# A graph network's last layer: fp32r halves for its weights, GpSimd for their products, PSUM for the running maximum

## The chip, the cores and the metric

The kernel runs on one core of one Trainium2 chip. The metric is the device time of one execution in microseconds (us); lower is better. TensorE multiplies matrices, VectorE and ScalarE work elementwise, GpSimd (POOL in the profile) too but without PSUM, and SyncE issues DMAs. Each engine runs its own instructions in order and waits for the others by semaphores.

## What is computed

Four graph layers work on 1354 nodes with 256 features. Each is `x = x + layer(relu(layernorm(x)), adj)`; the adjacency matrix `adj` is 1354 x 1354, F32, mostly zero. Layer 0 is softmax attention with `adj` added to the scores, layer 1 gated attention over neighbours, layer 2 a mean over neighbours. The change concerns layer 3:

```python
S = S + eye(n)                         # S is adj
h = x @ W
scores = where(S > 0, h @ U @ h.T, -inf)
att = softmax(scores, axis=-1)
return (S * att) @ h
```

## The kernel before

Nodes are cut into NB = 11 blocks of 128 (the last has 74). `adj` is stored transposed, so a tile has 128 neighbours (j) on the partitions and up to 512 target nodes in its columns. The targets form NG = 3 groups of 512, 512 and 330 columns, that is 4, 4 and 3 blocks. So there are NT = 33 tiles, numbered n = 11 * group + j. `slot3(n)` is the place in SBUF in which tile n's scores lie.

What layer 3 does for a tile, in the order of the data:

- TensorE, `score`: six fp32r matmuls make the scores in one of two PSUM banks. Layers 0 and 3 keep their operands as a high half, rounded to fp32r, and a low half, the rest; a product takes three matmuls (hi*hi, hi*lo, lo*hi; `products`, L309 to L311).
- VectorE, `add3` (L1322): masks with adj, negates, and writes the slot.
- VectorE, `running` (L912, L915): the running minimum of negated scores (the maximum, turned round) over the 11 tiles of a group, in `m_sb` in SBUF. When a group is complete, TensorE transposes `m_sb` (`turn_max`, L1490), VectorE reduces it (`top`, L894), and TensorE spreads the result over a PSUM bank (`spread_max`, L1499).
- VectorE, `shift` (L923): subtracts the group's maximum, from PSUM.
- ScalarE, `exp3` (L808): the exponential, in place.
- VectorE, `times_s` (L1330): times adj, into one of three places of `w_ring`, F32.
- GpSimd, `add_total` (L453): adds the exponentials of a group's tiles up in `total`. The first tile of a group is copied there by ScalarE (L812).
- TensorE, `aggregate3` (L1798): one F32 matmul for each of the group's blocks, weights times values, accumulated over the 11 tiles of the group. The profile has two records for each such F32 matmul.

At the end of a group `add_up` (L1814) sums `total` over partitions by matmuls with ones, and `out3` (L1338, L1344) divides and adds to x; SyncE stores each block.

The values `h @ W` are made in F32 in `v3` by ScalarE, from PSUM (`values`, L514). The layer's beginning is mixed with the end of layer 2 (`out2`, `turn_y`, `project2`) and with the normalisation of x.

The order is written by hand in a loop over steps s on each engine. In step s TensorE makes score s; VectorE takes it in `add3(s)` and shifts tile n at step `shift_step(n)`, which is n + 11 for the first group and n + 12 for the others. `times_s(n)` comes one step later and `aggregate3(n)` two steps later. The step count is NT + LAG3. Scores end with step 32; what comes behind is the tail, tiles 20 or so to 32. Layer 0 has the same shape of loop, with its weights in halves already: `weighted` (L1512, L1513 for the high part, L1517 for the low part) does three fp32r matmuls for each block.

## Time and profile before

| | |
|---|---|
| runs of the kernel | 415.62, 415.60, 414.38 us; median 415.6 |
| profiled execution, its own time | 415.22 us |
| its span in the trace | 413.4 us |
| busy of the span | TensorE 95%, VectorE 80%, ScalarE 53%, GpSimd 22% |
| mean granted TensorE clock | 0.996 of full speed |
| DMA queues | mean 34 GB/s; nearly idle after the first 40 us |

The span is what the trace covers, from the first instruction to the last; the time of the same execution has some 1.8 us more around it. The trace gives a start and a duration for each instruction. Matmuls overlap, so their spacing, not their duration, says what one costs.

### The profile page before, as it was taken

To read this page: it belongs to the slowest core of one execution; us is meant where nothing else is said; L and a number is where in the kernel's file an instruction comes from. 1 tells how busy PE (TensorE), PEld (TensorE's weight loads), DVE (VectorE), ACT (ScalarE), POOL (GpSimd) and SP (SyncE) were. 2 spreads that over 40 slices of the span, in tenths; PEclk is the share of its full clock that TensorE was granted. 3 is DMA by queue.
4 is the path that set the end of the run, shared out by engine and by line. 5 is a ranking of instruction groups with operands and counts; after the bars stand their busy time and mean duration, and the time that the engine had idled before them with its cause. 6 is when DMAs were issued, how large, how long until landed. Compare 5 with 4: busy or idle time off the path is not lost.

```text
span 413.4 us, 7338 instructions
## 1 busy us (share of the span) xinstructions
PE 394.8 (95%) x2534; PEld 355.2 (86%) x2534; DVE 329.1 (80%) x761; ACT 220.7 (53%) x454; POOL 89.5 (22%) x105
## 2 busy tenths in 40 slices
PE   8999999999899999999989999999999999999995
PEld 6787779989889989999989989997887788889863
DVE  4799789989895756998998989765758778798763
ACT  1453799975777567786777893254232311122330
POOL 1191000000110233233031001051010034324552
PEclk9999999999999999999999999999999999999998
DMA  8993000000000001000000000000000000010011
GB/s 249 376 377 120 2 0 2 2 0 2 1 2 0 2 0 52 2 2 0 3 2 0 2 1 2 2 1 2 0 2 0 2 1 0 2 51 2 0 52 33
DMA packets 10300, 13.96 MB, mean 34 GB/s; under 512 B 644, under 2 KB 7192, under 8 KB 10264
## 3 DMA queue, kind: packets, MB, share of 16 engines
q1 hardware_dynamic: 10264, 13.49, 9.6%
q8 instruction: 21, 0.34, 0.4%
q14 instruction: 15, 0.12, 0.1%
HBM read 12.10 MB, written 1.39 MB: 33 GB/s over the span
## 4 chain that ended last, share of the span: by engine, by line
PE 72%; DVE 17%; issue 6%; ACT 2%; POOL 1%; DVEq 0%; POOLq 0%; ACTq 0%
PE ps L1798 9%; PE ps L1517 9%; PE ps L1512 8%; PE ps L1513 8%; PE ps L309 6%; PE ps L311 6%; PE ps L310 6%; PE ps L1431 4%; PE ps L1725 3%; PE ps L1724 3%; PE ps L1754 2%; DVE m_sb L915 2%; PE ps L1536 2%; DVE s_sb L885 2%; DVE p_lo L929 1%
## 5 line engine op out<-in xcount | busy, mean ns | idle before, releaser
L1512 PE MATMUL ps<-v_hi,p_hi 128*128 128x258 f32 (+3 forms) x242 | 64.5, 297 | 1.1 <-DVE x_sb L941 0.7
L1513 PE MATMUL ps<-v_lo,p_hi 128*128 128x258 f32 (+3 forms) x242 | 61.0, 281 | 0.0
L1798 PE MATMUL ps<-v,w_ring 128*128 128x256 f32 (+3 forms) x242 | 58.0, 385 | 1.3 <-DVE w_ring L1330 0.8
L1798 PEld LDWEIGHTS ps<-v,w_ring 128*128 128x128 f32 (+3 forms) x242 | 43.2, 186 | 11.1 <-DVE w_ring L1330 4.5
L376 POOL TENSOR_TENSOR mr_all<-mr_all,mhalf 128x4 f32<-128x4 f32 (+1 forms) x12 | 13.3, 1106 | 173.6 <-DVE mr_all L847 173.6
L1512 PEld LDWEIGHTS ps<-v_hi,p_hi 128*128 128x128 f32 (+3 forms) x242 | 44.6, 184 | 3.5 <-ACT p_hi L520 1.6
L808 ACT ACTIVATE s_sb<-s_sb 128x512 f32<-128x512 f32 (+3 forms) x30 | 17.3, 575 | 53.9 <-DVE s_sb L923 53.9
L1513 PEld LDWEIGHTS ps<-v_lo,p_hi 128*128 128x128 f32 (+3 forms) x242 | 44.7, 185 | 0.5
L453 POOL TENSOR_TENSOR total<-total,s_sb 128x512 f32<-128x512 f32 (+3 forms) x27 | 30.6, 1134 | 65.2 <-DVE w_ring L1330 65.2
L1517 PE MATMUL ps<-v_hi,p_lo 128*128 128x258 f32 (+3 forms) x242 | 40.4, 285 | 2.1 <-DVE p_lo L929 1.7
L923 DVE TENSOR_TENSOR s_sb<-s_sb,ps 128x512 f32<-128x512 f32 (+3 forms) x63 | 38.4, 611 | 0.8 <-PE ps L1499 0.7
L1517 PEld LDWEIGHTS ps<-v_hi,p_lo 128*128 128x128 f32 (+3 forms) x242 | 32.5, 185 | 3.4 <-DVE p_lo L929 2.5
L915 DVE TENSOR_TENSOR m_sb<-m_sb,s_sb 128x512 f32<-128x512 f32 (+3 forms) x51 | 33.0, 646 | 0.9
L413 POOL TENSOR_TENSOR mid_lo<-adjT_sb,mid_hi 128x512 fp32r<-128x512 f32 (+2 forms) x16 | 20.6, 1289 | 51.4 <-ACT mid_hi L628 51.4
L1512 PE MATMUL ps<-big_hi,mid_hi 128*128 128x258 f32 (+3 forms) x121 | 31.7, 293 | 0.0
L1513 PE MATMUL ps<-big_lo,mid_hi 128*128 128x258 f32 (+3 forms) x121 | 30.3, 281 | 0.0
L309 PE MATMUL ps<-mid_hi,v_hi 128*128 128x512 f32 (+3 forms) x66 | 28.7, 434 | 1.0 <-DVE s_sb L1322 1.0
L637 ACT ACTIVATE p_hi<-s_sb,minus_r 128x512 fp32r<-128x512 f32 (+3 forms) x33 | 22.1, 671 | 11.2 <-PE ps L1517 4.5
L1105 DVE SCALAR_TENSOR_TENSOR s_sb<-s_sb,sx 128x512 f32<-128x512 f32 (+3 forms) x33 | 26.0, 789 | 1.2
L1322 DVE SCALAR_TENSOR_TENSOR s_sb<-adjT_sb,ps 128x512 f32<-128x512 f32 (+3 forms) x30 | 18.5, 616 | 10.3 <-PE ps L311 10.0
L309 PE MATMUL ps<-mid_hi,big_hi 128*128 128x512 f32 (+3 forms) x66 | 25.2, 382 | 0.8 <-DVE mid_lo L866 0.8
L520 ACT ACTIVATE p_hi<-s_sb 128x512 fp32r<-128x512 f32 (+3 forms) x33 | 19.0, 576 | 13.0 <-DVE s_sb L923 12.8
(228 smaller groups left out, 1049.5 us busy)
## 6 DMA issues: line engine op xcount, KB each, us to landing
adjT_sb<-in_adjT_dram SPq DMA_DIRECT2D x1, 2816.0 KB, 16.5
adjT_sb<-in_adjT_dram SPq DMA_DIRECT2D x3, 768.0 KB, 9.7
adjT_sb<-in_adjT_dram SPq DMA_DIRECT2D x1, 1815.0 KB, 20.9
out_dram<-x_sb SPq DMA_DIRECT2D x10, 128.0 KB
x_sb<-in_x_dram SPq DMA_DIRECT2D x2, 512.0 KB, 5.2
adjT_sb<-in_adjT_dram SPq DMA_DIRECT2D x1, 512.0 KB, 11.4
rows_sb<-in_rows_dram SPq DMA_DIRECT2D x1, 385.0 KB, 11.0
s_sb<-in_wq_dram SPq DMA_DIRECT2D x1, 256.0 KB, 3.9
```

The source lines that it names most:

```text
L309: eng.matmul(out_ap, lhs[0], rhs[0], start=first, stop=False)
L310: eng.matmul(out_ap, lhs[0], rhs[1], start=False, stop=False)
L311: return eng.matmul(out_ap, lhs[1], rhs[0], start=False, stop=last)
L453: pool.tensor_tensor(r, r, slot3(n), ALU.add).then_inc(tot_add, 1)
L637: act.activation(ring(p_hi, n), sum1(n), ACT.Exp, bias=bias, scale=SLOPE - 1.0).then_inc(e_hi, 1)
L915: dve.tensor_tensor(m, m, mine(n), op).then_inc(s_max[a], 1)
L923: dve.tensor_tensor(mine(n), mine(n), ps[0:rows(j), bank, 0:CW[gi]], ALU.subtract).then_inc(s_sub[a], 1)
L1105: dve.scalar_tensor_tensor(out=sum1(n), in0=left[0:rows(j), gi, 0:CW[gi]], scalar=sx[0:rows(j), j, 0:1], in1=sum1(n), op0=ALU.add, op1=ALU ...
L1512: pe.matmul(out_ap, left_[0][0:k, n % RING, mine], right_[0][0:k, j, 0:cols_], start=(j == 0), stop=False)
L1513: pe.matmul(out_ap, left_[0][0:k, n % RING, mine], right_[1][0:k, j, 0:cols_], start=False, stop=False)
L1517: ins = pe.matmul(ps[0:rows(b), banks[b % PER], 0:cols_], left_[1][0:k, n % RING, mine], right_[0][0:k, j, 0:cols_], start=False, stop=(j ...
L1798: ins = pe.matmul(ps[0:rows(b), SUMS3[gi][b % PER], 0:D], w_ring[0:k, n % RING, mine], v3[0:k, j, :], start=(j == 0), stop=(j == NB - 1))
```

## The change

The last layer is changed in these ways; nothing of what is computed is meant to change beyond rounding.

- **Halves.** The weights are split into an fp32r high half (in `p_lo`, written by ScalarE) and a low half (`w_lo`, by VectorE), the values likewise (`g[0]`, `g[1]`). `aggregate3` does three fp32r matmuls for each block in place of one F32 matmul. To have the weights in PSUM for VectorE's subtraction, ScalarE copies them to bank 3 as well (`w_hi`).
- **GpSimd's weights.** The product with adj is made by GpSimd for all tiles of the first two groups, and for tiles 23, 26, 29 and 32 of the last; VectorE makes it for the seven others (`OWN_W`). The product goes to `full3`, three places in buffers that are free by then. GpSimd's order is product n, total n. The first total of a group is now an addition of the first two tiles, so ScalarE's copy is gone.
- **Maximum in PSUM.** For the second and third group the running minimum is held in the group's PSUM bank (`far`). Its first tile is put there by a second `add3` instruction. The tile with 74 rows comes ninth; the tile before it (j = 9, the tenth) is taken last, together with the move to `m_sb`.
- **Order.** `aggregate3` is three steps behind the shift in place of two (LAG3 15), `weights3_lo` two. The four sums of each of the first two groups lie in two banks (`SUMS3`), opened by a matmul with a row of zeros; the totals are in bank 2.
- Two pairs of semaphores of layer 0 become one semaphore each (`col_mm`, `col_set`), and buffers are laid out anew.

The core of the diff:

```diff
-LAG3 = 14
+LAG3 = 15
-SUMS3 = [[0, 1, 2, 3], [0, 1, 2, 3], [4, 5, 7]]
-TOTALS_BANK = 3
+SUMS3 = [[(0, 0), (0, D), (1, 0), (1, D)]] * 2 + [[(4, 0), (5, 0), (7, 0)]]
+TOTALS_BANK, COPY_BANK = 2, 3
+OWN_W = [n for n in range(2 * NB, NT) if n % 3 != 2]
...
+        totals = [t[:, :, :].rearrange("p c n -> p (c n)")[:, 0:BANK] for t in (raw_a, raw_b)]
+        w_full = [t.rearrange("p b d -> p (b d)") for t in (z_buf[:, 0:2, :], z_buf[:, 2:4, :], asa_sb[:, :, :])]
...
+            def weights3(n):                                   # GpSimd
+                pool.wait_ge(pf[1], n + 1)
+                pool.wait_ge(phi, NT + n - 2)
+                wait(pool, w_copied, n - 2)
+                pool.tensor_tensor(full3(n), slot3(n), adj_tile(n), ALU.mult).then_inc(w_set, 1)
             def add_total(n):
-                pool.wait_ge(w_set, n + 1)
-                if j:
-                    wait(pool, tot_add, 10 * gi + j - 1)
-                    r = total[0:rows(j), gi % 2, 0:CW[gi]]
+                pool.wait_ge(pf[1], n + 1)
+                r = totals[gi % 2][0:rows(j), 0:CW[gi]]
+                if j == 1:
+                    wait(pool, tot_mm, gi - 1)
+                    pool.tensor_tensor(r, slot3(n - 1), slot3(n), ALU.add).then_inc(tot_add, 1)
+                elif j > 1:
+                    pool.wait_ge(tot_add, 10 * gi + j - 1)
                     pool.tensor_tensor(r, r, slot3(n), ALU.add).then_inc(tot_add, 1)
             for n in range(NT):
+                if n not in OWN_W:
+                    weights3(n)
                 add_total(n)
...
+            def w_hi(n):                                       # ScalarE
+                w_done(act, n)
+                wait(act, agg[1], n - 2)
+                act.activation(ring(p_lo, n), full3(n), ACT.Copy).then_inc(phi, 1)
+                act.wait_ge(plo, NT + n)
+                act.activation(ps[0:rows(n % NB), COPY_BANK, 0:CW[n // NB]], full3(n), ACT.Copy).then_inc(w_copied, 1)
+            values(8, 1)
+            for n in range(NT):
+                exp3(n)
+                if n < 2:
+                    values(n + 9, 1)
+                if n:
+                    w_hi(n - 1)
+            w_hi(NT - 1)
...
+                if a and gi:                                   # VectorE, running
+                    far = ps[0:rows(j), B3.shifts[gi % 2], 0:CW[gi]]
+                    wait(dve, s_max[a], 10 * gi + min(j, 9) - 1 if j > 1 else 0)
+                    if j != 9:
+                        dve.tensor_tensor(far, far, mine(n), op).then_inc(s_max[a], 1)
+                    if j == 10:
+                        dve.wait_ge(s_max[a], 10 * gi + 9)
+                        wait(dve, mt_mm[a], gi - 1)
+                        dve.tensor_tensor(m_sb[:, gi % 2, 0:CW[gi]], ps[:, B3.shifts[gi % 2], 0:CW[gi]], mine(n - 1),
+                                          op).then_inc(s_max[a], 1)
...
+                if gi and j == 0:                              # VectorE, add3
+                    dve.scalar_tensor_tensor(out=ps[:, B3.shifts[gi % 2], 0:CW[gi]], in0=adj_tile(n), scalar=0.0,
+                                             in1=ps[:, B3.scores[n % 2], 0:CW[gi]], op0=ALU.is_le, op1=ALU.subtract)
...
             def times_s(n):
                 dve.wait_ge(pf[1], n + 1)
-                wait(dve, agg[1], n - 2)
-                dve.tensor_tensor(ring(w_ring, n), slot3(n), adj_tile(n), ALU.mult).then_inc(w_set, 1)
+                dve.wait_ge(phi, NT + n - 2)
+                dve.wait_ge(w_copied, n - 2)
+                dve.tensor_tensor(full3(n), slot3(n), adj_tile(n), ALU.mult).then_inc(w_own, 1)
+            def weights3_lo(n):
+                dve.wait_ge(phi, NT + n + 1)
+                dve.wait_ge(w_copied, n + 1)
+                wait(dve, agg[1], n - 2)
+                dve.tensor_tensor(ring(w_lo, n), ps[0:rows(n % NB), COPY_BANK, 0:CW[n // NB]], f(ring(p_lo, n)),
+                                  ALU.subtract).then_inc(plo, 1)
+            def values3_lo(b):
+                r, bank = rows(b), B3.values[b % 2]
+                dve.wait_ge(vhi[1], b + 1)
+                dve.tensor_tensor(g[1][0:r, b, 0:D], ps[0:r, bank, 0:D], f(g[0][0:r, b, 0:D]), ALU.subtract).then_inc(vlo, 1)
...
                 running(s, 1, ALU.min)
+                if s < 8:
+                    values3_lo(s)
...
             shift(0, 1)
-            shift(1, 1)
-            add3(12)
-            times_s(0)
-            running(12, 1, ALU.min)
-            for s in range(13, NT + LAG3 - 1):
+            dve.memset(f(spare_mask[0:1, :]), 0.0)
+            values3_lo(8)
+            for s in range(12, NT + LAG3 - 1):
                 for gi in range(1, NG):
                     if s == NB * gi + (12 if gi == 1 else 11):
                         top(gi, 1, ALU.min)
-                if s == 24:
-                    times_s(11)
-                    out3(0)
-                if s == 37:
-                    out3(1)
-                if s < NT:
-                    add3(s)
                 if s < 22:
                     for n in tiles_at(s, 0):
                         shift(n, 1)
                 if s < NT:
+                    add3(s)
                     running(s, 1, ALU.min)
-                for n in tiles_at(s, 1):
-                    if n != 11:
-                        times_s(n)
+                if s < 14:
+                    values3_lo(s - 3)
                 if s >= 22:
                     for n in tiles_at(s, 0):
                         shift(n, 1)
+                for n in tiles_at(s, 1):
+                    if n in OWN_W:
+                        times_s(n)
+                for n in tiles_at(s, 2):
+                    weights3_lo(n)
+                if s == 24:
+                    out3(0)
+                if s == 37:
+                    out3(1)
...
-                pe.wait_ge(w_set, n + 1)                       # TensorE, aggregate3
+                pe.wait_ge(phi, NT + n + 1)
                 for b in blocks(gi):
-                    if n == NB:
-                        pe.wait_ge(x_add[3], b - PER + 1)
+                    if gi < 2 and j == 0 and b % 2 == 0:
+                        wait(pe, x_add[3], b - PER + 2)
+                        pe.matmul(ps[:, SUMS3[gi][b % PER][0], :], g[0][0:1, 0, 0:P], spare_mask[0:1, :], start=True, stop=False)
                     mine = slice((b % PER) * P, (b % PER) * P + rows(b))
-                    ins = pe.matmul(ps[0:rows(b), SUMS3[gi][b % PER], 0:D], w_ring[0:k, n % RING, mine], v3[0:k, j, :],
-                                    start=(j == 0), stop=(j == NB - 1))
+                    pe.matmul(sum3(b), p_lo[0:k, n % RING, mine], g[0][0:k, j, 0:D], start=(gi == 2 and j == 0),
+                              stop=False)
+                    pe.matmul(sum3(b), p_lo[0:k, n % RING, mine], g[1][0:k, j, 0:D], start=False, stop=False)
+                pe.wait_ge(plo, NT + n + 1)
+                for b in blocks(gi):
+                    mine = slice((b % PER) * P, (b % PER) * P + rows(b))
+                    ins = pe.matmul(sum3(b), w_lo[0:k, n % RING, mine], g[0][0:k, j, 0:D], start=False,
+                                    stop=(j == NB - 1 and (gi == 2 or b % 2 == 1)))
...
-                for n in tiles_at(s, 2):
+                for n in tiles_at(s, 3):
                     aggregate3(n)
```

## Rows read from the trace of the kernel before

**Rows 1.** The page, part 1: busy us, share of the span and instructions
```profile
PE 394.8 (95%) x2534; PEld 355.2 (86%) x2534; DVE 329.1 (80%) x761; ACT 220.7 (53%) x454; POOL 89.5 (22%) x105
```
**Rows 2.** Windows, a stretch of two steps: length, busy of each engine, clock, DMA
```profile
344.00:350.00 6.00, 6.00 (x29) 5.11 (x28) 4.98 (x8) 1.26 (x2) 2.32 (x3) 1.00 0.00 0
```
**Rows 3.** The chain that ended last, from 350 us on, by line
```profile
by line: PE ps L1798 40.6%; issue 8.3%; DVE s_sb L923 5.6%; ACT s_sb L808 5.3%; PE ps L311 4.9%; PE ps L309 4.9%; PE ps L310 4.9%; DVE x_sb L1344 4.3%; PE ps L1814 3.7%; DVE w_ring L1330 2.8%; POOLq L99 1.4%; DVE s_sb L1322 1.4%; POOL total
```
**Rows 4.** Timeline of TensorE: start, us, engine, line, operands, [idle before <-releaser]
```profile
344.09 1.89 PE L1798 MATMUL ps<-v,w_ring 128*128 128x256 f32 x8
345.62 0.58 PE L309 MATMUL ps<-mid_hi,v_hi 128*128 128x512 f32 x1
346.04 0.40 PE L310 MATMUL ps<-mid_lo,v_hi 128*128 128x512 f32 x1
...
347.21 1.89 PE L1798 MATMUL ps<-v,w_ring 128*128 128x256 f32 x8
...
372.70 1.89 PE L1798 MATMUL ps<-v,w_ring 128*128 128x256 f32 x8
...
375.33 1.89 PE L1798 MATMUL ps<-v,w_ring 128*128 128x256 f32 x8
```
**Rows 5.** Timeline of VectorE, the first instruction of one step
```profile
350.52 0.69 DVE L1322 SCALAR_TENSOR_TENSOR s_sb<-adjT_sb,ps 128x512 f32<-128x512 f32 x1 [0.63 <-PE ps L311]
```
**Rows 6.** Timelines of VectorE and ScalarE in the tail
```profile
399.11 0.49 DVE L923 TENSOR_TENSOR s_sb<-s_sb,ps 128x330 f32<-128x330 f32 x1
...
400.15 0.50 DVE L1330 TENSOR_TENSOR w_ring<-s_sb,adjT_sb 128x330 f32<-128x330 f32 x1 [0.55 <-ACT s_sb L808]
400.57 0.49 DVE L923 TENSOR_TENSOR s_sb<-s_sb,ps 128x330 f32<-128x330 f32 x1
...
399.64 0.48 ACT L808 ACTIVATE s_sb<-s_sb 128x330 f32<-128x330 f32 x1 [0.98 <-DVE s_sb L923]
```
**Rows 7.** Timelines of TensorE and GpSimd at the end of groups 1 and 2
```profile
391.75 2.84 PE L1798 MATMUL ps<-v,w_ring 128*128 128x256 f32 x12
...
407.49 0.74 PE L1814 MATMUL ps<-ones,total 128*128 128x1 f32 x6 [0.26 <-POOL total L453]
...
406.55 0.88 POOL L453 TENSOR_TENSOR total<-total,s_sb 74x330 f32<-74x330 f32 x1 [0.57 <-DVE w_ring L1330]
```
**Rows 8.** Timeline of TensorE in layer 0, aggregate and score of one step
```profile
91.85 0.28 PE L1512 MATMUL ps<-v_hi,p_hi 128*128 128x258 f32 x1
...
93.27 0.31 PE L309 MATMUL ps<-mid_hi,big_hi 128*128 128x330 f32 x1
...
94.19 0.28 PE L1512 MATMUL ps<-v_hi,p_hi 128*128 128x258 f32 x1
```
**Rows 9.** Timelines at the layer's start: TensorE, VectorE, ScalarE
```profile
315.16 0.47 PE L309 MATMUL ps<-mid_hi,v_hi 128*128 128x512 f32 x1 [1.01 <-DVE s_sb L1322]
...
322.25 0.69 DVE L894 TENSOR_REDUCE mx<-ps 128x4 f32<-128x512 f32 x1
...
324.40 0.63 ACT L808 ACTIVATE s_sb<-s_sb 128x512 f32<-128x512 f32 x1 [1.06 <-DVE s_sb L923]
```
**Rows 10.** Groups by line and shape from 300 us: busy, mean ns, idle before
```profile
L453 POOL TENSOR_TENSOR total<-total,s_sb 128x512 f32<-128x512 f32 x15 | 19.2, 1278 | 55.7 <-DVE w_ring L1330 55.7
L923 DVE TENSOR_TENSOR s_sb<-s_sb,ps 128x512 f32<-128x512 f32 x17 | 11.5, 680 | 0.7 <-PE ps L1499 0.7
...
L453 POOL TENSOR_TENSOR total<-total,s_sb 128x330 f32<-128x330 f32 x9 | 8.0, 890 | 7.6 <-DVE w_ring L1330 7.6
```
**Rows 11.** Timeline of GpSimd in layer 0, ten instructions in a row
```profile
22.75 8.66 POOL L385 TENSOR_TENSOR x_sb<-x_sb,rows_sb 128x256 f32<-128x256 f32 x10
```
**Rows 12.** Timelines where GpSimd and VectorE overlap; GpSimd's group of layer 1
```profile
356.21 1.27 POOL L453 TENSOR_TENSOR total<-total,s_sb 128x512 f32<-128x512 f32 x1 [1.83 <-DVE w_ring L1330]
...
356.69 1.33 DVE L1330 TENSOR_TENSOR w_ring<-s_sb,adjT_sb 74x512 f32<-74x512 f32 x1
...
L413 POOL TENSOR_TENSOR mid_lo<-adjT_sb,mid_hi 128x512 fp32r<-128x512 f32 x10 | 15.1, 1512 | 24.8 <-ACT mid_hi L628 24.8
```

76 lines of the change are left out of this document (37 added, 39 removed).

## The prediction

> **What bounds the kernel now.** I began with the page's busy shares: TensorE works for 95% of the span [rows 1]. An average says little about one layer, so I took a stretch of the last one next: TensorE is full, VectorE at 4.98 of 6.00 us, ScalarE at 1.26 (two exponentials, 0.63 each), GpSimd at 2.32, and the granted clock is 1.00, the 2.4 GHz level [rows 2]. The chain of waits says who sets the time: from 350 us on, 40.6% of it is the matmul L1798 (weights times values), and what follows is spread thin [rows 3].
>
> Then the timeline of TensorE. One step of the layer is one `aggregate3` and one score. While the scores have 512 columns it goes 344.09, 345.62, 347.21: a step of 3.12 us, 1.53 for the aggregate (eight records, four F32 matmuls) and 1.59 for the score. Its first matmul keeps TensorE 0.42 (345.62 to 346.04), the other five 0.234 each (to 347.21), so the F32 form leaves 0.18 behind. With scores of 330 columns the step is 372.70 to 375.33, 2.63 us [rows 4]. VectorE goes through its four instructions of a step and then stands for 0.63 us until TensorE delivers; 3.12 less 0.63 less the last 0.68 leaves three starts of 0.60 [rows 5]. So these 22 steps are TensorE's.
>
> The tail is another machine. From 389 us no scores are left and a tile goes by every 1.46 us: VectorE's shift 399.11, ScalarE's exponential 399.64, VectorE's product with adj 400.15, next shift 400.57, each waiting for the one before [rows 6]. TensorE's share of such a tile is three blocks, 1.53 x 3/4 = 1.15 us. The tail ends with the total of tile 32 on GpSimd at 406.55 and the column sums at 407.49; the last store lands with the span's end, 413.4 [rows 7].
>
> **The change on TensorE.** `aggregate3` becomes three fp32r matmuls a block for one F32. Layer 0 of this same kernel runs that form, with 258 columns for 256: from 91.85 to the next score at 93.27, and the next tile at 94.19 [rows 8]. So the aggregate costs 1.42 us with nothing late behind it, and a step with a 330 score 2.34. With a 512 score it is 1.42 + 6 x 0.234 = 2.82. Saved: 11 x (3.12 - 2.82) + 11 x (2.63 - 2.34) = 6.5 us. The four products with a zero row that open the shared banks are new, 512 columns each: 4 x 0.234 = 0.9 us.
>
> **What it puts on the others, and whether they hold the pace.** In the 512 step VectorE keeps add3, maximum and shift; the product goes to GpSimd, and `weights3_lo` takes its place. Add3 and maximum now stand side by side and the second waits for the first: its full 0.68 and a hand-over of 0.04 (399.11 + 0.49 to 399.64) in place of 0.60 [rows 6]. So 3 x 0.60 + 0.72 = 2.52 against 2.82. In the 330 step, by the start spacing of 0.42 (400.15 to 400.57), it is 0.53 + 0.42 + 0.60 + 0.60 = 2.15 against 2.34. It fits, without much room. A VectorE instruction that writes PSUM is not in the trace. The nearest rows, with PSUM only read, take 0.68 [rows 10]. I take that; from below nothing under 0.60 a start; from above I allow twice, 1.36. ScalarE: exponential and two copies, 3 x 0.63 = 1.9 us at most; its copy into PSUM has no row either, and I take the same: even at double, 2.5, it is under the long step and 0.2 over the short one.
>
> GpSimd gets the product besides the total: 2 x 1.28 = 2.56 us a tile [rows 10], if its instructions follow each other without a gap, as ten did in layer 0 (8.66 us for ten) [rows 11]. That is under 2.82 and over 2.34. Over both stages: 22 products and 20 totals, 42 x 1.28 = 53.8 us. It can begin when the first exponential is done, 324.40 + 0.63 [rows 9] plus the delay below, 325.9, so it could be through at 379.7, and TensorE needs it until about 387. The tile without a total at the head of a group gives back 1.28 us, six steps of the excess of 0.22. So I cost it at nothing, hidden by TensorE; without that cover it is 11 x 0.22 = 2.4 us.
>
> **The start of the layer.** From 311 to 321 us VectorE sets the pace: TensorE stood 1.01 us for its add3 at 315.16 [rows 9]. `values3_lo` adds 256 columns a block, under the 0.42 of 330: 0.35. Those of blocks 0 to 5 fall into time in which VectorE waits, that of block 6 is on the path (+0.35), that of block 7 I count as absorbed by the score after it. The second add3 of tile 11, into PSUM, lies straight ahead of `top` at 322.25 [rows 9], which also waited a little for TensorE: +0.5. Together +0.85 us; if block 7 and the whole 0.68 count, 1.4.
>
> Stalls: `out3(0)` now comes behind shift and maximum, and the last maximum of a group needs one more dependent instruction (0.53). I add 0.5, between 0 and the 2.0 of four new such places. Group 1's column sums ended at 391.75 [rows 7]; now 391.75 + 0.85 - 6.5 + 0.9 + 0.5 = 387.5.
>
> **The tail.** Its pace is now nobody's alone. ScalarE: three instructions of 0.48 [rows 6], 1.2 to 1.45. VectorE: shift, product (7 tiles of 11), low part, 3 x 0.42 = 1.26. GpSimd: 4 products and 10 totals, 14 x 0.89 = 12.5 us [rows 10], and it starts late, since it has still to finish tile 21 (its exponential near 383, product and total 2.56): 385.6. GpSimd and VectorE also get in each other's way. The product L1330 at 356.69 took 1.33 us for 0.68 and ended 0.54 after GpSimd's 356.21 + 1.27; and in layer 1, GpSimd's own instruction of that shape took 1.51 in the mean, beside VectorE's [rows 12]. So two instructions with both operands in SBUF exclude each other. Of VectorE's in this layer only the seven products of the last group are such (shift, add3, `weights3_lo` and the later maxima have an operand in PSUM). I give 7 x 0.3 = 2.1, between 0 and 7 x 0.50 = 3.5. Hand-overs, 14 x 0.06 = 0.8. GpSimd's last total ends at 385.6 + 12.5 + 0.8 + 2.1 = 401.0 and the product of tile 32 at 400.05; its high part 0.48, copy 0.48 and low part 0.50 follow, with 0.15 of hand-overs: 401.65. Then 0.2 to the column sums, and from them to the end 413.4 - 407.5 = 5.9 as before [rows 7]: 407.8. The tail shrinks little, because 14 GpSimd instructions cost what 11 tiles of 1.46 did, and because three more links hang behind the last product.
>
> Sum: the span of 413.4 becomes 407.8, 5.6 less. The profiled execution took 415.22, so 409.6 for its like; it lies 0.4 under the median of 415.6, so 410.0 against the median.
>
> The Trainium skill, GPSIMD Engine Reference, section 4.1, sends elementwise work to VectorE, as GpSimd is about twice as slow on two inputs; the trace agrees (1.28 against 0.68), and this speaks against giving it the product. Section 1 of that page says that GpSimd's SBUF interfaces contend with VectorE instructions that have two SBUF inputs; [rows 12] agree. By that rule too the two stages are free of it, and the last group is not.
>
> **The rivals.**
> 1. *TensorE is paid, but part is given back*: GpSimd or VectorE 0.22 a step behind in the second stage (2.4 us) and the whole 3.5 of exclusion in place of 2.1: 410.0 + 2.4 + 1.4 = 413.8. For it: three engines within 0.3 us of each other. Against: the tile without a total at each group's head.
> 2. *GpSimd paces everything: slower.* In layer 1 it took 1.51 in the mean for this shape [rows 12]. At 1.58 the 42 instructions end at 325.9 + 66.4 = 392.3 and the 14 (in proportion 1.10, and 0.06 of hand-over) at 408.5; less 1.16 for the last total, plus 1.6 + 0.2 + 5.9 for the chain of tile 32, is a span of 415.0, 417.2 on the median. It decides from about 1.55. Against: in layer 1 VectorE's partners had both operands in SBUF, here not.
> 3. *Nothing to measure*: VectorE's write to PSUM costs 1.2 in place of 0.68. Then the steps are 3.0 and 2.7, VectorE's, and both stages stand as before: 415.
> 4. *The tail is quick*: no exclusion (2.1) and the stalls and hand-overs hidden (1.0): 410.0 - 3.1 = 406.9.
>
> **How the numbers follow.** The forecast (408.5 to 412) has 0.50; rival 1 (412 to 414.3) 0.20; rival 4 (under 408.5) 0.13; rival 3 0.08; rival 2 0.09. About 0.3%, 1.2 us, is what a measurement of this kernel can tell from no change. So faster is 0.83, same 0.08, slower 0.09. The range 406.5 to 413.8 leaves out rivals 2 and 3 and the outer edges of 1 and 4, some 0.2.
>
> **What would show it.** In the profile after: matmuls of `aggregate3` 0.12 apart, steps of 2.8 and 2.35 us, idle TensorE under 2 us in both stages; GpSimd at 1.28 and over 85% busy from 327 to 386; VectorE's maxima with PSUM at 0.68, its products in the tail stretched to 0.8 and more; column sums of group 1 near 387.5, of group 2 near 401.9. The forecast is wrong if steps stay at 2.6 and over (the releaser of TensorE's idle time then names the engine), if a VectorE write to PSUM is over 1.1, or if the tail runs at 1.6 a tile or more.

## The result and the profile after

The kernel after takes 413.46 us (median of 15 executions, 412.39 to 414.37), the kernel before, beside it, 415.56 (15, 414.25 to 416.18). The ratio is 0.9958, with a 95% interval of 0.9945 to 0.997: 0.4% faster, and more than a measurement needs to tell it from no change. The forecast was 410.0. The direction is right and the time is inside the range, but of the 5.6 us that should go, 2.1 came.

The profiled execution of the kernel after took 414.33 us, its span 412.5. First the page, part 1, to be read against [rows 1]:

```profile
PE 391.0 (95%) x2659; PEld 357.5 (87%) x2659; DVE 337.6 (82%) x782; ACT 250.5 (61%) x517; POOL 118.5 (29%) x131
```

TensorE is 3.8 us less busy, GpSimd 29 us more. The windows of the stretch of [rows 2] (length, busy of PE, PEld, DVE, ACT, POOL, clock, DMA):

```profile
344.00:350.00 6.00, 6.00 (x41) 5.49 (x40) 5.48 (x10) 3.85 (x7) 5.27 (x5) 1.00 0.01 3
```

TensorE is still full there, VectorE is at 91% and GpSimd went from 2.32 to 5.27 of 6 us. The timeline of TensorE, one step with 512-column scores, for [rows 4]:

```profile
336.17 0.40 PE L324 MATMUL ps<-mid_hi,v_hi 128*128 128x512 f32 x1
...
337.58 0.28 PE L1862 MATMUL ps<-big_hi,p_lo 128*128 128x256 f32 x1
337.69 0.28 PE L1864 MATMUL ps<-big_lo,p_lo 128*128 128x256 f32 x1
...
338.51 0.63 PE L1868 MATMUL ps<-big_hi,w_lo 128*128 128x256 f32 x4
338.98 0.39 PE L324 MATMUL ps<-mid_hi,v_hi 128*128 128x512 f32 x1
```

A step is 338.98 - 336.17 = 2.81 us, an aggregate 1.40: as forecast (2.82, 1.42). So the steps themselves were paid. What sets the time has changed, though. The chain of waits from 350 us on, by line, for [rows 3]:

```profile
by line: issue 22.0%; POOL raw_b L478 8.3%; POOL raw_a L478 7.3%; ACT p_lo L840 5.8%; POOL asa_sb L466 5.7%; PE ps L1868 4.5%; ACT ps L842 3.3%; DVE more L966 3.1%; POOL z_buf L466 2.3%; DVE s_sb L966 2.1%; PE ps L1862 2.1%; POOL raw_b L475
```

Before, one matmul line held 40.6% of it. Now GpSimd holds at least 8.3 + 7.3 + 5.7 + 2.3 = 23.6%, with totals (L478) and products (L466), and no line of TensorE over 4.5%. ("issue", 22.0%, is time in which the engine next in the chain waited for nothing that the profile shows.) The timelines at the ends of groups 1 and 2 (TensorE; then GpSimd) for [rows 7]:

```profile
388.69 0.39 PE L1862 MATMUL ps<-big_hi,p_lo 74*128 74x256 f32 x1
...
390.24 0.74 PE L1868 MATMUL ps<-big_hi,w_lo 74*128 74x256 f32 x4 [0.33 <-DVE w_lo L1384]
390.81 0.95 PE L1884 MATMUL ps<-ones,raw_b 128*128 128x1 f32 x8
391.63 0.36 PE L1862 MATMUL ps<-big_hi,p_lo 128*128 128x256 f32 x1
...
406.61 0.64 PE L1884 MATMUL ps<-ones,raw_a 128*128 128x1 f32 x6
...
385.44 1.29 POOL L478 TENSOR_TENSOR raw_b<-raw_b,s_sb 128x512 f32<-128x512 f32 x1
386.69 1.28 POOL L466 TENSOR_TENSOR z_buf<-s_sb,adjT_sb 74x512 f32<-74x512 f32 x1
...
404.00 0.90 POOL L466 TENSOR_TENSOR asa_sb<-s_sb,adjT_sb 74x330 f32<-74x330 f32 x1
404.85 0.91 POOL L478 TENSOR_TENSOR raw_a<-raw_a,s_sb 74x330 f32<-74x330 f32 x1
```

Group 1's column sums are done at 391.63, where 387.5 was forecast and 391.75 was before. GpSimd ends at 405.76 instead of 401.0. One more thing was no part of the forecast at all. Windows of the kernel after, then of e4, a variant that does the same work up to there (same columns):

```profile
363.00:366.00 3.00, 3.00 (x12) 2.67 (x10) 2.97 (x7) 1.33 (x3) 2.32 (x2) 0.50 0.47 153
```

```profile
363.00:366.00 3.00, 3.00 (x17) 2.18 (x16) 2.97 (x8) 1.14 (x3) 2.33 (x2) 1.00 0.52 172
```

In this execution TensorE was granted the 1.2 GHz level for some 3.5 us, and from the first of two scores to tile 11's products it took 3.46 us (362.56 to 366.02), in e4 2.01 (362.17 to 364.18). By their mean clock I take it that this happened in 6 of the 15 executions: 6 are at 0.994 or less and take 414.0 in the mean, 9 are at 0.997 or more and take 413.15.

For the experiments I cut the layer at fixed points of TensorE's timeline: the transposes of the first maximum, the column sums of groups 0, 1 and 2, and the end of the span. Lengths in us, from the start of one to the start of the next, in the profiled executions (the span's end is known to 0.1 us). One execution of e1 took 539.97 us at a mean clock of 0.653 and is left out everywhere.

| kernel | to sums 0 | to sums 1 | to sums 2 | to the end | ratio to before (95%) |
|---|---|---|---|---|---|
| before | 39.73 | 29.63 | 16.55 | 5.91 | 1 |
| after | 39.52 | 29.06 | 15.80 | 5.89 | 0.9958 (0.9945 to 0.997) |
| e1 | 38.82 | 29.40 | 15.33 | 5.83 | 0.9957 (0.994 to 0.9974) |
| e2 | 38.47 | 28.50 | 15.79 | 5.90 | 0.9934 (0.9917 to 0.9951) |
| e3 | 39.00 | 28.51 | 15.76 | 5.88 | 0.9962 (0.9939 to 0.9985) |
| e4 | 39.54 | 28.50 | 15.64 | 5.80 | 0.9953 (0.9935 to 0.9971) |
| e5 | 39.53 | 29.11 | 15.80 | 5.90 | 0.9954 (0.9942 to 0.9966) |
| e6 | 47.93 | 31.62 | 15.84 | 5.85 | 1.0242 (1.0229 to 1.0256) |
| e7 | 39.58 | 32.51 | 15.79 | 5.85 | 1.006 (1.0047 to 1.0074) |
| e8 | 38.11 | 28.53 | 15.69 | 5.87 | 0.9919 (0.9905 to 0.9933) |
| e9 | 39.54 | 27.71 | 15.16 | 5.87 | 0.9914 (0.9899 to 0.993) |
| e10 | 39.54 | 29.06 | 15.78 | 5.88 | 0.9972 (0.9961 to 0.9984) |
| e11 | 38.08 | 28.27 | 14.96 | 5.87 | 0.9895 (0.9878 to 0.9912) |
| e12 | 37.39 | 28.27 | 14.95 | 5.80 | 0.9884 (0.9867 to 0.9901) |
| e13 | 39.51 | 26.88 | 14.18 | 5.83 | 0.9897 (0.9876 to 0.9918) |
| e14 | 37.37 | 26.88 | 13.91 | 5.86 | 0.9826 (0.981 to 0.9843) |
| e15 | 37.38 | 27.67 | 14.95 | 5.78 | 0.9869 (0.985 to 0.9887) |
| e16 | 37.41 | 27.71 | 14.96 | 5.80 | 0.9876 (0.9861 to 0.9891) |
| e17 | 37.41 | 27.71 | 15.07 | 5.85 | 0.9871 (0.9852 to 0.989) |

The first point itself lies between 321.0 and 322.4 in all of these, with no edit of theirs before it; that much varies ahead of the layer. The kernel after reaches it at 322.23, before at 321.58.

The stretches of before and after hold different work, since `aggregate3` now comes a step later. One more score of 330 columns, that of tile 24, stands ahead of group 0's sums; it starts at 358.74 in the kernel after and behind the sums in the kernel before, and takes 0.9 us (six matmuls 0.15 apart).

```profile
358.74 0.31 PE L324 MATMUL ps<-mid_hi,v_hi 128*128 128x330 f32 x1
...
359.49 0.31 PE L326 MATMUL ps<-mid_hi,v_lo 128*128 128x330 f32 x1
```

The forecast in these terms: the first point at 321.58 + 0.35 = 321.93; to sums 0, 39.73 less 11 aggregates at 0.30, plus 0.9 for that score, 0.5 for the second masked copy (it lies behind the first point), 0.47 for two bank-opening products and 0.25 for half of the stalls, is 38.55; to sums 1, 29.63 less 11 at 0.29, less 0.9, plus 0.47 and 0.25, is 26.26; to sums 2, 16.55 less the 1.34 that the tail was to lose (15.74 to 14.4), is 15.2.

| | first point | to sums 0 | to sums 1 | to sums 2 |
|---|---|---|---|---|
| forecast | 321.93 | 38.55 | 26.26 | 15.2 |
| kernel after | 322.23 | 39.52 | 29.06 | 15.80 |
| too long by | 0.3 | 1.0 | 2.8 | 0.6 |

So most of what is missing lies between group 0's and group 1's sums.

### The profile page after: what moved, and what is told of

Same layout as the page of the kernel before. It is cut to its first block and busy times, and to the rows that moved or that the text cites. A ratio compares the mean times of both kernels' runs of the same rounds, so it can differ in the third digit from the quotient of the medians.

```text
span 412.5 us, 7764 instructions
## 1 busy us (share of the span) xinstructions
PE 391.0 (95%) x2659; PEld 357.5 (87%) x2659; DVE 337.6 (82%) x782; ACT 250.5 (61%) x517; POOL 118.5 (29%) x131
## 5 line engine op out<-in xcount | busy, mean ns | idle before, releaser
L1862 PE MATMUL ps<-big_hi,p_lo 128*128 128x256 f32 (+3 forms) x121 | 31.6, 292 | 0.3
L1864 PE MATMUL ps<-big_lo,p_lo 128*128 128x256 f32 (+3 forms) x121 | 30.4, 282 | 0.0
L324 PE MATMUL ps<-mid_hi,v_hi 128*128 128x512 f32 (+3 forms) x66 | 26.0, 395 | 1.3 <-DVE s_sb L1368 1.3
L1155 DVE TENSOR_TENSOR p_lo<-s_sb,p_hi 128x512 fp32r<-128x512 f32 (+3 forms) x33 | 21.8, 659 | 3.9 <-ACT s_sb L665 3.9
L325 PE MATMUL ps<-mid_lo,v_hi 128*128 128x512 f32 (+3 forms) x66 | 24.9, 377 | 0.0
L326 PE MATMUL ps<-mid_hi,v_lo 128*128 128x512 f32 (+3 forms) x66 | 24.9, 377 | 0.0
```

What stands on the lines that cost most here:

```text
L324: eng.matmul(out_ap, lhs[0], rhs[0], start=first, stop=False)
L325: eng.matmul(out_ap, lhs[0], rhs[1], start=False, stop=False)
L326: return eng.matmul(out_ap, lhs[1], rhs[0], start=False, stop=last)
L1155: dve.tensor_tensor(ring(p_lo, n), sum1(n), f(ring(p_hi, n)), ALU.subtract).then_inc(e_lo, 1)
L1862: pe.matmul(sum3(b), p_lo[0:k, n % RING, mine], g[0][0:k, j, 0:D], start=(gi == 2 and j == 0), stop=False)
L1864: pe.matmul(sum3(b), p_lo[0:k, n % RING, mine], g[1][0:k, j, 0:D], start=False, stop=False)
```

## The experiments

All edits are to the kernel after. In each expectation A is the theory that what the edit takes away costs time (in e6 and e7, that the edit itself does), B the rival. Where products move to VectorE, the waits that go with them are changed too and not printed.

**e1, ScalarE's order at the group ends.** In the kernel after the rounded half of tile 10 waits from 353.15, when its product is there, to 359.25, behind the exponential of tile 11, which waits for the next group's maximum.

```diff
             for n in range(NT):
+                first = n in (NB, 2 * NB)
+                if first:
+                    w_hi(n - 1)
                 exp3(n)
...
-                if n:
+                if n and not first:
                     w_hi(n - 1)
```

> ScalarE takes the rounded half of tile 10 (and of tile 21) before the exponential of tile 11 (22), and not behind it. Theory A, the order of ScalarE's work at the two group ends is what holds the last products of a group up: the high copy of tile 10 comes at about 353.5 instead of 359.25, the products of tile 10 and 11 no longer meet idle time, and TensorE has no stretch at the lower clock level between 362 and 366; the span falls by 1.5 to 3, to 409.5 to 411. Theory B, the two-score stretch at half clock comes by itself and tile 21 waits for GpSimd's product (started at 386.69) in either order: the time stays within 0.5 us of the kernel after.

Measured: 413.4, ratio 0.9957, no gain. All five executions were at a mean clock of 0.991 or less, so the clock has a part in this. The first stretch got 0.7 shorter. The second did not, for two reasons that its trace shows. VectorE (timeline):

```profile
385.38 0.49 DVE L969 TENSOR_TENSOR s_sb<-s_sb,ps 128x330 f32<-128x330 f32 x1
387.56 0.50 DVE L1380 TENSOR_TENSOR z_buf<-s_sb,adjT_sb 128x330 f32<-128x330 f32 x1 [1.69 <-ACT s_sb L834]
387.98 0.68 DVE L1387 TENSOR_TENSOR w_lo<-ps,p_lo 74x512 fp32r<-74x512 f32 x1
```

With the exponential of tile 22 moved back, VectorE's product of tile 22 waits 1.69 us for it, and the low half of tile 21, queued behind, comes no earlier. And the clock was at the lower level from about 388 to 396 instead of 363 to 366 (0.58 and 0.57 in the windows 388 to 392 and 392 to 396). Theory A holds at the end of group 0 and fails at the end of group 1.

**e2, no bank-opening products.** The first product of the even block opens the bank; the odd block's first one goes on without a start flag.

```diff
-                        pe.matmul(ps[:, SUMS3[gi][b % PER][0], :], g[0][0:1, 0, 0:P], spare_mask[0:1, :], start=True, stop=False)
...
-                    pe.matmul(sum3(b), p_lo[0:k, n % RING, mine], g[0][0:k, j, 0:D], start=(gi == 2 and j == 0),
+                    pe.matmul(sum3(b), p_lo[0:k, n % RING, mine], g[0][0:k, j, 0:D], start=(j == 0 and (gi == 2 or b % 2 == 0)),
```

> The four one-row products that clear a whole bank are gone; the first product of the even block of each bank starts the bank instead. Theory A, the zeroing products cost what a 256-column product costs twice over, 0.23 each (my forecast): 0.9 us less at most. Theory B, they cost more, since the step of tile 0 took 3.24 against 1.42 for a plain one: tile 0's step falls to about 2.1 (the wait for the low parts of the values stays), 1.0 there and 0.5 to 1.0 at tile 11: 1.5 to 2 us less in all. If they hide behind the waits at those two places: nothing, within 0.4 us.

Measured: 412.16, ratio 0.9934, so 1.0 us less than the kernel after by the ratios. The first stretch is 1.05 shorter. TensorE at tile 0, in the kernel after:

```profile
330.78 0.46 PE L1860 MATMUL ps<-spare_mask,big_hi 1*128 1x512 f32 x1 [0.55 <-issue]
331.17 0.38 PE L1862 MATMUL ps<-big_hi,p_lo 128*128 128x256 f32 x1
331.40 0.28 PE L1864 MATMUL ps<-big_lo,p_lo 128*128 128x256 f32 x1
...
331.84 0.49 PE L1860 MATMUL ps<-spare_mask,big_hi 1*128 1x512 f32 x1
332.26 0.38 PE L1862 MATMUL ps<-big_hi,p_lo 128*128 128x256 f32 x1
```

and in e2:

```profile
330.48 0.35 PE L1861 MATMUL ps<-big_hi,p_lo 128*128 128x256 f32 x1 [0.50 <-issue]
330.67 0.28 PE L1863 MATMUL ps<-big_lo,p_lo 128*128 128x256 f32 x1
...
331.50 0.63 PE L1867 MATMUL ps<-big_hi,w_lo 128*128 128x256 f32 x4
```

From the first product of the tile to its low-half products it is 332.84 - 330.78 = 2.06 us with two such products and 1.02 without: 0.52 each, not 0.234. A 1-row, 512-column product keeps TensorE 0.39 to 0.42, and the product behind it starts slowly too (0.23 to the next start instead of 0.12). At tile 11 the gain is hidden: there TensorE then waits 1.22 us for the low half of tile 11, and the second stretch is 28.50 as in e4. Theory A's price at tile 0 was 0.47 for two; B's, 1.0, is what the rows show.

The Trainium skill, PSUM — Partial Sum Buffer, "The four PSUM rules", says that a matmul with the start flag clears the written marks of the whole bank and that an unflagged one overwrites where they are clear. By that rule the opening products are not needed, and e2 agrees: it computes the same sums without them.

**e3, tile 0 waits for the low parts of the values block by block.**

```diff
                 if n == 0:
-                    pe.wait_ge(vlo, 2 * NB)
+                    pe.wait_ge(vlo, NB + 8)
                     h_done(pe, 3, NB)
...
                 for b in blocks(gi):
+                    if n == 0 and b == 2:
+                        pe.wait_ge(vlo, 2 * NB)
```

> Tile 0's products of the first two blocks wait for nine low parts of the values only; all eleven are wanted from the third block on. Theory A, that wait costs the 0.55 to 0.7 us that TensorE idles at 330.1: 0.5 us less. Theory B, it only moves to the third block, or the following tiles wait for halves of the weights anyway: no change, within 0.3 us.

Measured: 413.08, ratio 0.9962. Its first stretch is 0.5 shorter, as A says, but its executions spread from 411.9 to 416.8 with mean clocks from 0.998 down to 0.978, and the ratio shows no gain. Its three executions at 0.997 or more took 411.9 to 412.2, against 413.15 for those of the kernel after; but the kernel before took 415.11 beside e3 and 415.56 beside the kernel after, so 0.45 of that is not e3's. So 0.5 is likely, not shown.

**e4, the output blocks of group 1 one to a step.**

```diff
-                if s == 37:
-                    out3(1)
+                if 37 <= s < 41:
+                    out3(1, s - 37)
```

`out3` takes the number of the block as a second argument.

> The four output blocks of group 1 go one to a step of VectorE (steps 37 to 40) instead of all four at once in step 37. Theory A, the block of 1.58 us at 393.23 stops ScalarE (idle 1.74) and GpSimd (2.42) in the tail where VectorE sets the pace only in part: 0.5 to 1.2 us less, since these engines go on. Theory B, the tail is VectorE's own sum of work, or GpSimd's, and the order within it is worth nothing: within 0.3 us.

Measured: 413.05, ratio 0.9953; the tail took 15.64 for 15.80. Theory B: that ScalarE stands 1.74 and GpSimd 2.42 us there costs next to nothing in the end. Up to sums 1 e4 is the kernel after at full clock, so its 28.50 serves below as that kernel's second stretch without the lower level.

**e5, all products of the last group on VectorE.**

```diff
-OWN_W = [n for n in range(2 * NB, NT) if n % 3 != 2]
+OWN_W = list(range(2 * NB, NT))
```

> VectorE multiplies all eleven tiles of the last group (tiles 23, 26, 29 and 32 too, which GpSimd had); GpSimd only adds totals there. Theory A, the tail runs at GpSimd's pace (my forecast's step: last total at 401.0), and its four products of 1.3 us are what makes it late: the tail gets 0.5 to 1.5 us shorter, since tile 32's halves no longer wait for GpSimd. Theory B, VectorE sets the pace of the tail (busy 9.63 of 10 us in 390 to 400): four more instructions of 0.50 with 0.3 of waiting each are put on it, 1.5 to 3 us more.

Measured: 413.15, ratio 0.9954, tail 15.80 as in the kernel after. Neither theory: GpSimd gives up 3.3 us of products, VectorE's go from 5.6 to 7.9, and the tail keeps its length.

**e6, all 33 products on VectorE.** GpSimd's products are undone, the rounded halves stay.

```diff
-OWN_W = [n for n in range(2 * NB, NT) if n % 3 != 2]
+OWN_W = list(range(NT))
...
-                    dve.wait_ge(w_set, k + 1)
+                    w_done(dve, k)
```

> VectorE multiplies all 33 tiles; GpSimd only adds totals. The part of the change that gives products to GpSimd is undone, the rounded halves stay. Theory A, VectorE's work for a step is 2.55 us now (9.05 of 10 us busy in 340 to 350) and a product of 0.69 brings it to 3.25, over TensorE's 2.82: some 0.4 us on each of 12 to 20 steps, 5 to 8 us more than the kernel after, so slower than the kernel before. Theory B, VectorE has that much room, since GpSimd now keeps it waiting less: within 2 us of the kernel after.

Measured: 425.16, ratio 1.0242, 10 us slower than before. Theory A, and more than it said. The timeline of GpSimd's total, then of VectorE, one step:

```profile
339.03 1.29 POOL L478 TENSOR_TENSOR raw_a<-raw_a,s_sb 128x512 f32<-128x512 f32 x1 [2.49 <-ACT s_sb L834]
...
339.53 1.35 DVE L1377 TENSOR_TENSOR z_buf<-s_sb,adjT_sb 128x512 f32<-128x512 f32 x1
340.80 0.68 DVE L1384 TENSOR_TENSOR w_lo<-ps,p_lo 128x512 fp32r<-128x512 f32 x1
341.40 0.67 DVE L966 TENSOR_TENSOR s_sb<-s_sb,ps 128x512 f32<-128x512 f32 x1
342.00 0.67 DVE L1368 SCALAR_TENSOR_TENSOR more<-adjT_sb,ps 128x512 f32<-128x512 f32 x1
342.70 0.70 DVE L947 TENSOR_TENSOR ps<-ps,more 128x512 f32<-128x512 f32 x1
343.31 1.34 DVE L1377 TENSOR_TENSOR z_buf<-s_sb,adjT_sb 128x512 f32<-128x512 f32 x1
```

The step is 3.78 us. A product that takes 0.68 alone (tile 21's in e14) takes 1.35 beside GpSimd's total, and ends 0.56 after it (340.88 against 340.32). Without these 0.67 the step would by my estimate be 3.11, still over TensorE's 2.82. The rounded halves without GpSimd's products make this kernel slower.

**e7, the maximum of groups 1 and 2 in SBUF.** `running` takes the first group's branch for all groups, and the second masked copy of `add3` goes.

```diff
-                if gi and j == 0:
-                    dve.scalar_tensor_tensor(out=ps[:, B3.shifts[gi % 2], 0:CW[gi]], in0=adj_tile(n), scalar=0.0,
-                                             in1=ps[:, B3.scores[n % 2], 0:CW[gi]], op0=ALU.is_le, op1=ALU.subtract)
...
-                if a and gi:
-                    far = ps[0:rows(j), B3.shifts[gi % 2], 0:CW[gi]]
...
-                elif j == 1:
+                if j == 1:
```

The rest of the branch `if a and gi` goes as well.

> The running maximum of the second and third group stays in SBUF, as for the first group and as in the kernel before; the additional masked copy into PSUM at the start of these groups is gone. Theory A, an instruction of VectorE with two operands in SBUF is held up while GpSimd works (products took 0.80 instead of 0.50 in the last group): the maximum takes 0.69 plus 0.3 to 0.8 instead of 0.70, VectorE's step goes from 2.55 to about 3.0 in the steps of tiles 12 to 21, and the time rises by 1 to 3 us. Theory B, VectorE has 0.27 us of slack in a step and the two additional copies are saved: no change or 0.5 less.

Measured: 417.6, ratio 1.006: 4.1 us over the kernel after, slower than before. Theory A, larger than its bound. The groups by line and shape from 325 us on, in e7 (busy us, mean ns):

```profile
L948 DVE TENSOR_TENSOR m_sb<-m_sb,s_sb 128x330 f32<-128x330 f32 x8 | 9.1, 1141 | 0.3
L948 DVE TENSOR_TENSOR m_sb<-m_sb,s_sb 128x512 f32<-128x512 f32 x5 | 5.0, 997 | 0.2
...
L466 POOL TENSOR_TENSOR z_buf<-s_sb,adjT_sb 128x512 f32<-128x512 f32 x11 | 15.4, 1402 | 26.8 <-ACT s_sb L834 26.8
```

and in the kernel after:

```profile
L947 DVE TENSOR_TENSOR ps<-ps,s_sb 128x330 f32<-128x330 f32 x8 | 4.1, 510 | 0.3
L947 DVE TENSOR_TENSOR ps<-ps,s_sb 128x512 f32<-128x512 f32 x5 | 3.5, 700 | 0.2
...
L466 POOL TENSOR_TENSOR z_buf<-s_sb,adjT_sb 128x512 f32<-128x512 f32 x11 | 13.1, 1190 | 27.2 <-ACT s_sb L834 27.2
```

With one operand in PSUM the maximum takes 0.51 and 0.70; with both in SBUF 1.14 and 1.00 beside a busy GpSimd, and GpSimd's product is drawn out as well, 1.19 to 1.40. The Trainium skill, GPSIMD Engine Reference, section 1, names this contention for VectorE instructions with two SBUF inputs; e6 (1.35 for 0.68) and e7 (1.14 for 0.51 with a PSUM operand) agree. In e7 the first point to the spreading of the first maximum is 1.41 us, as before, and 1.78 in the kernel after: the second masked copy costs 0.37 there.

**e8, e2 to e4 together.**

> The edits of e2 (no zeroing products), e3 (first products wait for nine low parts only) and e4 (output blocks of group 1 one to a step) together. Theory A, they act at three places of the path and add up: e2 gave 1.3 us less than the kernel after by the medians, e3 and e4 0.3 to 0.4 each, so about 2 us less, 411 to 411.5. Theory B, what is gained before 390 is given back where tile 21 waits for GpSimd's product and in a stretch at the lower clock, as e1's 1.5 us of its profile were in the medians: no better than e2 alone, 412.2.

Measured: 411.94, ratio 0.9919, 1.6 us less than the kernel after by the ratios. The first stretch adds up (1.05 and 0.5 expected, 1.41 measured); the second, 28.53, is that of e2 and e4 alone. What e2 takes away at tile 11 is hidden there by the wait for tile 11's low half.

**e9, tile 21's product on VectorE.**

```diff
-OWN_W = [n for n in range(2 * NB, NT) if n % 3 != 2]
+OWN_W = [21] + [n for n in range(2 * NB, NT) if n % 3 != 2]
```

> VectorE multiplies tile 21, the last of group 1, and GpSimd keeps the others. In the kernel after GpSimd starts this product at 386.69, 0.7 us after its exponential, and TensorE's last products of the group start at 388.69. Theory A, GpSimd is what is late at the end of group 1: VectorE (idle 0.9 us there) delivers it about 1.2 earlier, the column sums of group 1 come 0.7 to 1.2 earlier and the span falls by as much. Theory B, the instruction of VectorE is itself held up by GpSimd's work on the total (as the product of tile 22 was, 1.50 instead of 0.50) and holds up the shifts behind it: within 0.4 us.

Measured: 411.33, ratio 0.9914, 1.8 us less by the ratios, the largest gain of any single edit that leaves the work whole. The second stretch is 27.71 against 28.50 in e4, where the clock was full too, and the tail 15.16 against 15.64. The column sums, in e9:

```profile
388.14 0.69 PE L1868 MATMUL ps<-big_hi,w_lo 74*128 74x256 f32 x4
388.67 0.95 PE L1884 MATMUL ps<-ones,raw_b 128*128 128x1 f32 x8
```

The wait ahead of the last low-half products is gone; one of 0.50 now stands ahead of tile 20's. Theory A, though the product itself took 1.57 us beside GpSimd's total.

**e10, the low half of tile 11 right after the output blocks of group 0.**

```diff
                 for n in tiles_at(s, 2):
-                    weights3_lo(n)
+                    if n != 11:
+                        weights3_lo(n)
                 if s == 24:
                     out3(0)
+                    weights3_lo(11)
```

> The low half of tile 11's weights, the first of group 1, is taken right after the four output blocks of group 0 and not behind the next masked copy, maximum and shift. Theory A, TensorE waits for that half once the zeroing products are gone (1.21 us in e8's trace at 364.4), in the kernel after these products and the half clock hide it: within 0.4 us here, and 0.7 to 1.2 less only in e11. Theory B, VectorE sets the pace at the start of group 1 in either kernel: nothing in both.

Measured: 413.78, ratio 0.9972: no gain, and second stretch 29.06 at full clock against 28.50 in e4. The masked copy behind it comes later; that this is the cause is not shown.

**e11, e8 with e9 and e10**, and **e12, e11 with e1's order at the end of group 0 alone** (`first = n == NB`).

> The three edits of e8 with those of e9 and e10. Theory A, they act at five places one after the other: e8 measured 411.9; with 1.0 from the low half of tile 11 and 0.7 to 1.2 from tile 21, 410 to 410.3, which is what I had forecast for the kernel after. Theory B, GpSimd (10.00 of 10 us busy in 370 to 380) or VectorE takes up what TensorE gains: 411.5 to 412.

> e11 with ScalarE's order changed at the first group end alone: the rounded half of tile 10 before the exponential of tile 11; the order at the end of group 1, where e1 put a wait of 1.69 on VectorE, stays. Theory A, e1 gained 1.5 us up to 390 in its trace and lost it there and to the lower clock level: 0.5 to 1 less than e11. Theory B, TensorE waits for nothing of it at that place (idle 0.3): within 0.3 us of e11.

Measured: e11 410.51, ratio 0.9895; e12 410.02, ratio 0.9884. The intervals of the two overlap, but the stretch that e12's edit touches is 0.7 shorter (37.39 for 38.08), as e1's was. e11 was at the lower clock level for 3.4 us soon after sums 0, e12 at full clock, and both have 28.27 in the second stretch: as far as these two tell, the lower level cost nothing there.

**e13 and e14, totals on 8 columns only**, in the kernel after and in e12. This leaves out the normalising sums of all other columns.

```diff
-                r = totals[gi % 2][0:rows(j), 0:CW[gi]]
+                r, w = totals[gi % 2][0:rows(j), 0:8], slice(0, 8)
...
-                    pool.tensor_tensor(r, r, slot3(n), ALU.add).then_inc(tot_add, 1)
+                    pool.tensor_tensor(r, r, slot3(n)[:, w], ALU.add).then_inc(tot_add, 1)
```

> The kernel after with the sums for the totals cut to their first 8 columns, so that GpSimd has its 26 products and next to no additions; this leaves out the normalising sums of all other columns. Theory A, GpSimd's total of 1.3 us ahead of each product is what makes the last products of group 1 late and holds VectorE's products up in the tail: product(21) starts at its exponential, the products of the last group take 0.50, and the time falls by 3 to 4.5, to 409 to 410.5. Theory B, GpSimd is in the way only at tile 21: as e9, 411.3.

> The same cut in the kernel e12. Theory A, e12 still pays for GpSimd: its product of tile 21 on VectorE takes 1.83 and GpSimd is 10.00 of 10 us busy in 370 to 380; 1.5 to 2.5 less than e12, 407.5 to 408.5. Theory B, e12 has taken out what GpSimd costs, and TensorE and VectorE set its time: within 0.5 of e12's 410.0.

Measured: e13 410.47, ratio 0.9897, 2.5 us less than the kernel after; e14 407.9, ratio 0.9826, 2.4 less than e12. Theory A in both; in e13 a little less than it said. Groups by shape, e13:

```profile
L478 POOL TENSOR_TENSOR raw_a<-raw_a,s_sb 128x8 f32<-128x8 f32 x16 | 3.2, 203 | 3.5 <-ACT s_sb L834 3.5
...
L1377 DVE TENSOR_TENSOR z_buf<-s_sb,adjT_sb 128x330 f32<-128x330 f32 x7 | 3.5, 496 | 0.0
```

and the kernel after:

```profile
L478 POOL TENSOR_TENSOR raw_a<-raw_a,s_sb 128x330 f32<-128x330 f32 x8 | 7.6, 953 | 1.2 <-POOL raw_a L478 0.5
...
L1377 DVE TENSOR_TENSOR z_buf<-s_sb,adjT_sb 128x330 f32<-128x330 f32 x7 | 5.6, 802 | 0.0
```

The first stretch does not change (39.51): up to there GpSimd really is hidden. The second is 26.88, where 26.26 was forecast, and the tail 14.18.

**e15, e12 with tile 17's product on VectorE too**; **e16, e15 without e10's edit**; **e17, e16 without e4's**.

```diff
-OWN_W = [21] + [n for n in range(2 * NB, NT) if n % 3 != 2]
+OWN_W = [17, 21] + [n for n in range(2 * NB, NT) if n % 3 != 2]
```

> e12 with the product of tile 17 on VectorE too. In steps of 330-column scores TensorE takes 2.36 us and GpSimd 1.30 + 1.19 for a tile of 512 columns, so GpSimd falls behind by some 0.13 a step from tile 11 on. Theory A, one product less lets GpSimd catch up before the end of group 1: 0.3 to 0.8 less than e12. Theory B, VectorE (9.2 of 10 us busy in 370 to 380) has no room for another 0.69 and a wait of up to 1.1: 0 to 1 more.

> e15 without the edit of e10: the low half of tile 11 again behind the masked copy, maximum and shift. From the start of group 0's column sums to that of group 1's e9 took 27.71 us, e10 29.06, e4 (neither edit) 28.50, e15 27.67. Theory A, e10's edit costs some 0.5 us there, since masked copy and shift come later for it: 0.3 to 0.6 less than e15, 409.2 to 409.5. Theory B, it only costs that beside the zeroing products: within 0.2 of e15's 409.75.

> e16 with the output blocks of group 1 all at once again, as in the kernel after. Theory A, where they stand is worth nothing: e4's tail took 15.64 us against 15.80; within 0.3 of e16. Theory B, once GpSimd is less of a bound in the tail, their block of 1.66 us shows: 0.5 or more over e16.

Measured: 409.75 (0.9869), 409.67 (0.9876) and 409.67 (0.9871). e15 is 0.6 less than e12 by the ratios, with intervals that overlap, and its second stretch is 0.6 shorter, as theory A says. But e9 has 27.71 there with neither this edit nor e10's, and e16 27.71 with this one alone, so that the 0.6 may be no more than what e10's edit had cost e12; with tile 17 on VectorE it costs nothing (27.67 with it, 27.71 without). e16 itself goes to its theory B, within 0.2 of e15, and e17 to its theory A: the place of the output blocks is worth nothing. e17, with the edits of e2 and e3, e1's at the end of group 0 and the products of tiles 17 and 21 on VectorE, is as good as any that leaves the work whole: 1.3% faster than the kernel before, 0.9% than the kernel after.

## Why the forecast was right in direction and too large

- **Steps of TensorE, 6.5 us saved**: right. 2.81 us and 2.36 (373.31 to 375.67) against 2.82 and 2.34.
- **VectorE writing PSUM, taken at 0.68**: right, 0.700. Rival 3 is out.
- **Start of the layer, +0.85**: measured +1.02 at the start of score 12 (323.40 before, 324.42 after): the first cut point lies 0.65 later, and the second masked copy adds 0.37. Right in size, as far as the variation ahead of it lets one say.
- **Zeroing products, 0.9**: mis-sized. 0.52 each at full clock (e2), 2.1 for four; the visible part is the 1.0 of tile 0, where I had 0.47.
- **Stalls, 0.5**: mis-sized. Tile 0's wait for all low values shows as 0.7 us between the last score's products and 330.78 (0.5 by e3's stretch), ScalarE's order at the end of group 0 costs 0.7 (e1, e12). I had a range of 0 to 2.0 for new waits and took its lower end, having looked only at `out3` and the last maximum. Reading each engine's new order at the group ends, line by line, would have found both.
- **GpSimd costed at nothing**: the step that failed. The sum let 42 instructions follow each other from 325.9 on and be through at 379.7. But none can start before its exponential, and at the turn to group 1 GpSimd stood for 5.03, 2.76 and 1.12 us, waiting for those of tiles 11, 12 and 13; nothing of this was in the sum:

```profile
359.42 1.28 POOL L466 TENSOR_TENSOR asa_sb<-s_sb,adjT_sb 128x512 f32<-128x512 f32 x1 [5.03 <-ACT s_sb L834]
363.45 1.09 POOL L466 TENSOR_TENSOR z_buf<-s_sb,adjT_sb 128x512 f32<-128x512 f32 x1 [2.76 <-ACT s_sb L834]
...
366.90 1.28 POOL L466 TENSOR_TENSOR z_buf<-s_sb,adjT_sb 128x512 f32<-128x512 f32 x1 [1.12 <-ACT s_sb L834]
```

From there on the tiles come every 2.36 us and its work on one is 1.30 + 1.19 = 2.49, so it can only lag; the tile without a total gives its 1.3 us at the head, where nothing is waiting. In the kernel after it is 9.63 of 10 us busy in 370 to 380, and at the end tile 21's product starts at 386.69, behind the total of tile 20, and its total ends at 389.21. Against e4, e9 (one product away) gains 0.8 in that stretch and 0.5 in the tail, e13 (next to no totals) 1.6 and 1.5; of the 3.5 us between 410.0 and 413.46, e9 brings back 1.8 and e13 2.5. It is part of rival 1, not rival 2: no step is paced by GpSimd while TensorE has other work; it shows where TensorE runs out of it. The time lies in rival 1's band, for half of its reason: the lag came, the exclusion of 3.5 did not.
- **Exclusion in the tail, 7 x 0.3**: right, 0.802 against 0.496 in e13, 2.1 us in all. e6 and e7 show that the rest of the layout, products on GpSimd and the maximum with PSUM, is what keeps the layer free of it.
- **Tail, group 1's sums at 387.5 to group 2's at 401.9**: 14.4 us forecast, 406.61 - 391.63 = 14.98 measured. Slightly short. That GpSimd alone bounds it was too simple: e5, which frees it of four products, gains nothing.
- **The clock**: not in the forecast. The stretch at 1.2 GHz in mid-layer costs 1.45 us up to tile 11 in the profiled execution (3.46 for 2.01), but only 0.56 by group 1's sums (29.06 for 28.50), since GpSimd's lag then hides the rest: from the transposes of the third maximum to these sums it is 7.70 us in the kernel after and 8.41 in e4. 0.85 is the difference between the means of the executions at 0.994 and less and at 0.997 and more. e1, e2, e3 and e8 have a low mean clock in most of theirs. TensorE was 9.89 of 10 us busy in 350 to 360, before it fell; why it falls in some executions and not in others stays open.

Put together for the profiled execution, whose span is 4.7 us over the forecast (412.5 for 407.8): 0.3 ahead of the first point; 1.0 up to sums 0, where opening products, tile 0's wait and ScalarE's order cost 1.5 more than I had allowed and some 0.5 came back, 0.13 of it from the second masked copy, the rest unexplained; 2.8 up to sums 1, of which 1.6 is GpSimd (e13), 0.56 the clock, and some 0.6 stays open; 0.6 in the tail. The medians are only 3.5 over it, since the profiled execution lies 0.9 over its median and that of before 0.4 under. That the time came out inside the range owes something to luck: rival 1, which reaches so far, prices GpSimd's lag by the step and not its standstill at the turn.

## What to carry to other kernels

An engine whose work on a tile is within 0.1 to 0.3 us of another's step has no cover at a group's end. Don't add its work up from a start time: ask at each turn of a group when its inputs come (here it stood for 8.9 us). Lay out its last items, with the instruction that each is queued behind, and give the last one to whoever idles (e9: one tile, 1.8 us). When work moves to GpSimd, keep VectorE's instructions beside it to one SBUF operand; when it can't be, count up to GpSimd's whole instruction as the price. And look up what each queue has ahead of the last item of a group, since a reorder of one engine alone (e1) may only move the wait.
